# Six row searches of an image moved later in VectorE's written order, across a period's end

## What is computed

```
h = tok(x)                                  # 4x4 pixel blocks -> 256 tokens of 64 channels, local attention over the 16 pixels of a block
h = h + ssm(layernorm(h))                   # selective scan, forward and backward, 128 channels x 16 states, gated, projected
h = h + pk(layernorm(h))                    # product-key memory with 8 heads, then causal attention
# pk, for each token and head:
#   scores, idx = top_k(q @ keys, 16)       # two sides of 64 keys each
#   final_scores, pk_idx = top_k(all pairs of the two lists, 16)
#   rows = take_along_axis(pair indices, pk_idx)      # which 16 rows of a 4096-row table
#   k, v = softmax(final_scores) @ keys_table[rows], values_table[rows]
#   out  = causal_attention(q, k, v) @ Wo
```

## Time and profile before

| what | value |
|---|---|
| median of 3 runs | 12154.85 us (12135.15 to 12179.6) |
| the profiled execution, its own time | 12173.09 us |
| its span, first to last instruction | 12171.2 us |
| TensorE busy, VectorE busy, ScalarE busy, GpSimd busy | 87%, 84%, 65%, 70% |
| mean granted TensorE clock | 0.969 |

### The profile page before, as it was taken

The page is one execution under the profiler, slowest core; times in us unless marked ns, Lnnn a source line. Parts: engine busy times, 40 slices in busy tenths (PEclk is TensorE's granted clock), DMA queues, the critical chain, the costliest instruction groups (busy, mean ns, idle before and its releaser), DMA issues.

```text
span 12171.2 us, 265707 instructions
## 1 busy us (share of the span) xinstructions
PE 10589.8 (87%) x70908; PEld 7592.4 (62%) x70908; DVE 10219.5 (84%) x42190; ACT 7922.6 (65%) x18182; POOL 8492.6 (70%) x8196
## 2 busy tenths in 40 slices
PE   3888888888888888888888888888888888888888
PEld 2666666666666666666666666666666666666665
DVE  6888888888888888888888888988888888888883
ACT  2666666666666666666666666666666666666665
POOL 0777777677777676776776676777767767777676
PEclk6999999999999999999999999999999999999999
DMA  2566566566565565565665655655655556556554
GB/s 65 155 172 176 154 172 173 154 173 171 157 171 166 160 173 157 167 174 151 172 171 157 172 159 166 178 153 168 172 157 170 164 162 175 156 168 174 150 168 137
DMA packets 1651838, 1975.60 MB, mean 162 GB/s; under 512 B 336238, under 2 KB 1125870, under 8 KB 1649902
## 3 DMA queue, kind: packets, MB, share of 16 engines
q1 hardware_dynamic: 1387950, 1418.48, 40.2%
q0 software_dynamic: 262144, 537.40, 16.5%
HBM read 1881.20 MB, written 73.40 MB: 161 GB/s over the span
## 4 chain that ended last, share of the span: by engine, by line
PE 52%; DVE 18%; ACT 13%; issue 9%; DMA 6%; SPq 2%; POOL 0%; ACTq 0%; DVEq 0%; POOLq 0%
PE bank L1011 15%; PE bank L1034 6%; PE bank L1021 5%; ACT bank L1267 5%; PE bank L894 4%; PE bank L1046 4%; DVE decay L1602 4%; DMA wide<-states 4%; PE bank L998 2%; DVE onehot L1827 2%; ACT weight L1274 2%; PE bank L941 2%; PE bank L1070 2%; DMA moving<-keyspace 2%; PE bank L975 2%
## 5 line engine op out<-in xcount | busy, mean ns | idle before, releaser
L822 POOL DMA_INDIRECT gath<-in_table_dram,rowsT x8192 | 8492.4, 1037 | 3648.3 <-issue 2420.3
L1274 ACT ACTIVATE weight<-bank 128x512 f32<-128x512 f32 x4096 | 2443.1, 596 | 3030.3 <-PE bank L1021 3009.3
L1011 PE MATMUL bank<-weight,rowtab 128*128 128x256 f32 x16384 | 4298.5, 385 | 0.0
L1011 PEld LDWEIGHTS bank<-weight,rowtab 128*128 128x128 f32 x16384 | 3138.0, 193 | 741.6 <-issue 41.9
L1267 ACT ACTIVATE bank<-bank,seventeen 128x512 f32<-128x512 f32 x4096 | 2715.5, 663 | 14.7 <-PE bank L1021 11.6
L1034 PE MATMUL bank<-moving,pick_b 96*128 96x512 bf16 x4096 | 1600.2, 391 | 759.5 <-ACT bank L1267 643.8
L1021 PE MATMUL bank<-moving,pick_b 96*128 96x512 bf16 x4096 | 1572.2, 384 | 28.5 <-DMA moving<-keyspace 27.7
L1034 PEld LDWEIGHTS bank<-moving,pick_b 96*128 96x128 bf16 x4096 | 436.3, 107 | 1320.7 <-ACT bank L1267 1131.0
L1602 DVE TENSOR_TENSOR_SCAN decay<-decay,wide 128x256 f32<-128x256 f32 x2048 | 1237.3, 669 | 0.3
L1864 DVE SCALAR_TENSOR_TENSOR acc<-bank,rrow,acc 128x64 f32<-128x64 f32 x1024 | 240.8, 276 | 948.8 <-PE bank L1021 885.4
L1208 ACT ACTIVATE decay<-delta,a_neg 128x255 f32<-128x255 f32 x2048 | 867.6, 504 | 145.7 <-DVE mx L1583 145.7
(11 more groups left out here) (271 smaller groups left out, 17466.4 us busy)
## 6 DMA issues: line engine op xcount, KB each, us to landing
rowtab<-in_tableD_dram SPq DMA_DIRECT2D x2048, 256.0 KB
wide<-states SPq DMA_DIRECT2D x512, 512.0 KB, 4.6
moving<-keyspace SPq DMA_DIRECT2D x4096, 64.0 KB
gath<-in_table_dram,rowsT POOLq DMA_INDIRECT x8192
moving<-keyspace SPq DMA_DIRECT2D x4096, 32.0 KB
pix<-in_x_dram SPq DMA_DIRECT2D x504, 256.0 KB
keyspace<-split SPq DMA_DIRECT2D x256, 256.0 KB, 2.2
out_dram<-acc SPq DMA_DIRECT2D x64, 64.0 KB
```

The costliest lines, as they stand in the source:

```text
L822: pool.indirect_dma_start(out=gath[:, u % RING, j, :], out_offset=None, in_=table, in_offset=bass.IndirectOffsetOnAxis(ap=rowsT[k][:, col: ...
L1011: mm(dense_ps[:, 0:TOK], rowtab[:, r, s % 2 * 2 + half, :], weight[s % 2][:, half * TOK:(half + 1) * TOK], start=(s % 16 == 0 and half == ...
L1274: ins = af(weight[s % 2][:], zd_ps[s % 2][:], ACT.Exp, scale=-1.0)
```

## The change

Only the text of DVE_ORDER changes. R2 goes from row 46 to row 63. R3 goes from row 59, R4 and R5 from row 62 and R6 from row 63 into the next period, to rows 1, 6, 7 and 7, so their lead goes from +1 to +0. R7, which was in row 5 of that period already, goes to row 8. `a6.6` and `T0` go from row 7 to row 9 and with that behind all of them; their places among the other steps stay. No weight write (`wb`) changes its place, and no instruction is added or removed.

```
@@ DVE_ORDER
 0 F.y+1 a5.6-1
-1 F.ps+2 F.g+1
+1 F.ps+2 S.R3+0 F.g+1
 2 S.e6+0 S.e7+0
 3 F.h2+1 S.re3+0
 4 S.wb1+0
-5 a6.3-1 S.n0+1 S.n1+1 S.lo3+0 S.R7+0
-6 F.rf+2 a6.5-1
-7 a6.6-1 S.T0+1
-8 
-9 
+5 a6.3-1 S.n0+1 S.n1+1 S.lo3+0
+6 F.rf+2 a6.5-1 S.R4+0
+7 S.R5+0 S.R6+0
+8 S.R7+0
+9 a6.6-1 S.T0+1
...
 45 S.R1+1 F.sf0+2
-46 S.R2+1 a3.3+0
+46 a3.3+0
...
 58 S.A3+1 F.C3+2
-59 S.R3+1 a5.3+0
+59 a5.3+0
 60 
 61 S.wb0+1 S.e5+1 a5.5+0
-62 S.R4+1 S.lo2+1 S.R5+1
-63 S.R6+1
+62 S.lo2+1
+63 S.R2+1
```

## The result

The changed kernel took 12223.14 us (median of 4 runs, 12220.76 to 12231.2). Its ratio to the kernel before is 1.0056, with a 95% interval of 1.0037 to 1.0075: slower by 0.56%, some 68 us. The forecast was 12190 us in a range of 12125 to 12255, with 0.43 for slower, 0.44 for within 0.3% and 0.13 for faster. So the time lies in the range, 33 us over the forecast. The two profiled executions, 12173.09 and 12221.22 us, are 48 us apart.

The account below looks back on a forecast made before the run. The path changes hands, with TensorE holding 52% of the chain, so VectorE's moves matter only where another engine waits. Terms 58 - 24 - 2 - 5 + 8 = 35 us on the median 12154.85 gave 12190 us, range 12125 to 12255.

Parts of the forecast that it names:

- A: Likeliest case, the sum of all terms: R3 delays wout_g and TensorE waits at L957; 12145 to 12235 us, chance 0.60.
- case B: Nothing to be seen: F.bk's cost comes back at the keys and in later slack; 12155 us, chance 0.14.
- R3 into row 1: R3 between F.ps and F.g makes wout_g 2.50 us later for F.bk: 0.92 us a period, 58 us slower.
- What follows R3: Steps behind R3 in its stretch are also 2.50 us late, but their readers have room: cost 0.
- R4 to R7 and the excess of 0.5 us: Ahead of a6.6, 9.0 us of searches meet 8.52 us idle; TensorE's lateness covers the excess: 0, at worst 31 us.
- R2 out of row 46: VectorE's scan comes sooner, so slot 53's keys load sooner: 24 us faster, bounds 0 and 27.7.
- L941: TensorE's 89.0 us of waits for VectorE's C products: what S4 saves, S6 waits; 2 us faster.
- case D: Faster: waits at S4 to S7 hang on VectorE's full stretch, so TensorE regains 89.0 us; 12099 us, chance 0.12.
- The start: In the first periods, before TensorE sets the pace, VectorE's net work removed gives 5 us faster.
- The clock: The new stand at F.bk may bring a few half-clock stretches of 1.7 us: 8 us slower, bounds 0 and 107.
- Case C: Slower by more: TensorE's stand in row 3 brings half clock in every second period; 12235 us, chance 0.14.

Follow-up runs that it names:

- e3: The changed kernel with R3 ahead of a5.6 in row 0, not between F.ps and F.g: 12146.65 us, ratio 0.9987 to the kernel before.
- e1: The changed kernel with R2 left in row 46: 12235.92 us, ratio 1.0061 to the kernel before.
- e5: The kernel before with only R4 to R7 moved between a6.5 and a6.6: 12159.79 us, ratio 0.9999.
- e8: The changed kernel unaltered, rerun on a chip with a clock of 0.88: 15703.40 us, ratio 1.0085 to the kernel before.
- e9: The kernel of e3 (R3 between F.y and a5.6), rerun on the chip of e8: 15642.86 us, ratio 1.0044 to the kernel before.
- e11: The changed kernel with R3 behind F.g in row 1, on the chip of e8: 15698.72 us, ratio 1.0083 to the kernel before.
- e12: The kernel of e5 (only R4 to R7 moved), run again on a chip like the first: 12153.21 us, ratio 0.9994 to the kernel before.
- e2: The kernel before with only R2 moved, from row 46 to row 59 ahead of R3: 12203.41 us, ratio 1.0037.
- e7: The changed kernel with R3 behind R2 in row 63, on a second chip with a clock of 0.88: 15515.36 us, ratio 1.0074 to the kernel before.
- e10: The changed kernel with R3 behind R2 in row 63, ahead of F.y, on the chip of e8: 15637.68 us, ratio 1.0043 to the kernel before.

## Why the prediction was right, and where its sizes were off

**The mechanism** was the likeliest case, A. L957 waits for L1625 57 times and 65.5 us, inside the 50 to 60 times and 55 to 70 us that were named, and e3 shows that this place and no other carries the cost. The rule of the Trainium skill that stood beside case B (Perfetto Trace Analysis, Identifying the Most-Contended Engine), applied to an order-only change, is not borne out here: VectorE's occupancy stayed at 84%, and the time rose by 0.56%.

**R3 into row 1: 58 forecast.** The spare of F.bk was read rightly: a mean stand of 1.07 us against 1.06 worked out, with 0.13 given back at z3 against 0.16, and slot 3 is 0.87 longer, 55 us. (The working has a slip of 1 us: 1.06 less the 0.16 that it shows is 0.90, not 0.92.) The whole price of R3's place was larger, 76 us in both comparisons on the first chip (after less e3, e1 less e5) and 61 on the third (e8 less e9).

**What follows R3: put at nothing.** This is the step that failed: "it has more room than F.bk: nothing", said of S.E3. Slot 5 is 0.16 us longer, 63 x 0.16 = 10 us, by the delay of L998 behind `rest`; and e11 shows a stand of 0.93 us a period where F.bk's own stand does not cover it. S.E3 did have more room, but by 0.26 us only (1.79 against 1.53 in the kernel before), and R3 is 2.50 us long. ScalarE's S.n does wait more (95.5 us now), but w5 behind it still waits for TensorE and not for n0: ScalarE's idle time ahead of it fell from 1.65 to 0.57 us in the mean and did not run out, so that part held. GpSimd held too: TensorE waits 0.2 us for gathered rows from 340 to 12100 us, against 4.2 before, and no wait of GpSimd is put down to `rowsT` there.

**R4 to R7 and the excess of 0.5 us: 0 forecast.** e5 and e12 gave 0.9999 and 0.9994. VectorE's idle time ahead of a6.6 is gone, as it should be. What the term left out is the end: in the last two images L1070 waits 4.0 us for the `acc` of a6.6, and the stretch from the 63rd image's first o to the end is 3.5 us longer.

**R2 out of row 46: -24 forecast.** The keys' wait fell to 9.6 us, not under 8, and by 0.30 us a period at slot 53, or 19 us. But R2 has only part of that: the wait is 0.24 in e1, where R2 stays, against 0.12 with its move, and 0.43 in e5 against 0.26 and 0.24 in e2 and e3. That is 0.12 to 0.19 us a period, 8 to 12 us, and 13 us between the medians of e1 and after. The term was taken at nearly its upper bound, and R2's own part was worth half or less; that the keys gave 19 us all the same is luck. Why the keys wait less once R3 is in row 1, with R2 where it was, no run tells.

**L941: -2 forecast.** Slot 59 gained 0.19 and slot 61 lost 0.21: "What TensorE does not wait at S4 it waits at S6" held almost to the hundredth. This ruled out case D, whose 89.0 us did not move.

**The start: -5 forecast.** TensorE's first o came 3.0 us sooner (303.3 in place of 306.3), but that of the fifth image came at 1036.2 before and 1036.1 after. The gain was lost at once: 0. Two traces of one kernel, e5 and e12, differ by 1.0 and 2.4 us at these two points, so not even the 3.0 us is sure.

**The clock: +8 forecast.** Case C did not come: slot 3 has less half clock than before, by 0.37 us a period, and only 0.13 to 0.19 more than e5 and e3. Part of it turned up elsewhere. Slot 55 has 0.5 to 0.6 us a period more of it than the kernel before, and 1.0 to 1.2 more than e3 and e5 have, in both kernels with the stand at L957 (after and e1). Over all runs on these chips of which the clock is listed, the mean clock was 0.9703 before (42 runs) and 0.9692 after (4 runs), and within one kernel (before, e1, e2, e3, e5, e12) the time rises by 6 to 12 us for each 0.001 lost; that makes 7 to 13 us. In the two profiled executions it is 0.969 both times. That the stand at L957 causes it is only argued, and that the size is near the 8 us of the forecast, which stood for half clock in slot 3, is luck.

**The sum.** 55 for slot 3, 10 for slot 5, -19 for the keys (R2's part and the rest), 0 for L941 and the start, 4 for the last two images, and 7 to 13 for the clock make 57 to 63 us; 68 was measured between the medians, so 5 to 11 us have no place in this sum. Its terms are of two kinds, slots out of one execution each and the clock out of means over runs, so a gap of some us is no surprise. The forecast's 35 was too low by 33: S.E3's cost of 10 was put at nothing, the 5 us of the start did not come, the keys gave 5 less than was taken, the last two images cost 4, and the rest is what this sum leaves open. Against the profiled executions the miss is smaller: 12208 was worked out and 12221.22 came, 13 us over, since the one of before lay 18 us above its median and the one of after 2 under its own. That the change was slower by more than a measurement can miss had the chance of 0.43; within 0.3% had 0.44.

## What to carry to other kernels

Idle time on an engine can take up work only if the work stands ahead of it in that engine's order; one place behind it, the same step is paid in full beyond the spare of its nearest reader. So read, for a step to be moved, the room between the end of everything queued behind it and the readers of each, not only the first: here two readers had nearly the same room, 1.5 and 1.8 us, and taking the step from one showed the other. And before a search is taken out of a full stretch, ask whether TensorE waits there for VectorE or for what VectorE itself waits for: 6.5 us less work in rows 59 to 63 gained nothing.

## What the runs showed of the hardware that was not expected

The same kernel took 12158 and 12162 us on two jobs' chips and 15408 and 15571 us on two others. The clock's row of the page, for 40 slices, is in the first line the changed kernel's on a chip of the first kind:

```profile
PEclk6999999999999999999999999999999999999999
```

and here that of e9, with its wait of z for ScalarE over the whole execution:

```profile
PEclk7888888888888898888888888888888888888888
PE bank L1034 <- ACT bank L1267: 1697.3, 1044, 5.9
```

The same wait is 635.9 us in the changed kernel's profile on the first kind. TensorE's mean clock was 0.880 in place of 0.969; its granted clock was about half, the 1.2 GHz level, for 3658 us of e7's execution against 763 of before's. ScalarE's own instructions took the same (L1267: 663 ns in both), so the loss of 27 to 28% is far more than the extra half clock itself, some 1450 us: the steps that wait on each other across TensorE and ScalarE stretch too, and traces of these chips also lack many releasers. No run tells what sets these chips apart.

It matters for the verdict. The cost of R3's place held on both kinds (76 and 61 us), but the rest of the change, free or a gain of 0.13% on the first, cost 0.44% on the second (e9, e10), and 0.74% in e7. Half clock is one candidate: the mean clock over all runs was 0.8833 before and 0.8805 and 0.8808 in e9 and e10, and within these three kernels the time rises by 8 to 11 us for each 0.001 lost, which makes some 20 to 30 of the 72 and 67 us. R2 in row 63 is another. R4 to R7 ahead of a6.6 are a third, but against them stands that in the traces of e9 and e10 `acc` ends 0.6 us ahead of L1070 in slot 10 in the mean, and L1070 does not wait there in images 5 to 62. The run meant to split them landed on a chip of the first kind, and of the kernel before no trace was taken on these chips, so this stays open.
